# A graph network on one core: residual tiles reloaded earlier, last heads scaled one step ahead, scale weights split in another stage

## The reference, cut to what matters

```python
for i in range(4):
    y = cond_layer_norm(x, cond, s1_w[i], s1_b[i], b1_w[i], b1_b[i])      # xn * (1 + cond@sw + sb) + (cond@bw + bb)
    y = sparse_attention(y, src, dst, wq[i], bq[i], wk[i], bk[i], wv[i], bv[i], wo[i], bo[i])
    x = x + y
    y = cond_layer_norm(x, cond, s2_w[i], s2_b[i], b2_w[i], b2_b[i])
    x = x + relu(y @ m_w1[i] + m_b1[i]) @ m_w2[i] + m_b2[i]
```

## Time and profile before

| | |
|---|---|
| median of 3 runs | 1757.74 us (1755.12 to 1758.2) |
| the profiled execution: time | 1758.62 us |
| its span, first to last instruction | 1756.9 us |
| PE busy | 1718.3 us (98%) |
| DVE busy | 1210.8 us (69%) |
| ACT busy | 802.0 us (46%) |
| POOL busy | 555.4 us (32%) |
| mean granted TensorE clock | 0.995 |

### The profile page before, as it was taken

The page is one execution under the profiler, slowest core; times in us unless marked ns, Lnnn a source line. Parts: engine busy times, 40 slices in busy tenths (PEclk is TensorE's granted clock), DMA queues, the critical chain, the costliest instruction groups (busy, mean ns, idle before and its releaser), DMA issues.

```text
span 1756.9 us, 32326 instructions
## 1 busy us (share of the span) xinstructions
PE 1718.3 (98%) x11894; PEld 1516.8 (86%) x11894; DVE 1210.8 (69%) x2215; ACT 802.0 (46%) x1322; POOL 555.4 (32%) x887
## 2 busy tenths in 40 slices
PE   7999999999999999999999999999999999999998
PEld 6998788888999788889998888899988887999877
DVE  6996459457787765477777573677766836777685
ACT  4667332136666231256663412466634123666531
POOL 1002513313333722033337330233354402233473
PEclk9999999999999999999999999999999999999999
DMA  4003311311111313121113122112130312111221
GB/s 133 1 1 131 131 43 43 126 69 43 47 46 31 117 31 122 44 64 46 46 31 96 55 83 83 46 46 61 31 99 25 100 53 75 39 46 61 68 92 71
DMA packets 64714, 113.07 MB, mean 64 GB/s; under 512 B 15254, under 2 KB 25622, under 8 KB 64576
## 3 DMA queue, kind: packets, MB, share of 16 engines
q1 hardware_dynamic: 64576, 111.22, 19.3%
HBM read 89.19 MB, written 22.00 MB: 63 GB/s over the span
## 4 chain that ended last, share of the span: by engine, by line
PE 91%; DVE 4%; issue 2%; DMA 1%; POOL 1%; DVEq 1%; ACT 0%; ACTq 0%; SPq 0%; POOLq 0%
PE ps L1539 59%; PE ps L1599 15%; PE ps L1692 6%; PE ps L1489 4%; PE ps L1524 2%; PE ps L1624 2%; PE ps L1638 2%; DVE masked_s L1261 1%; DMA x<-in_x_dram 1%; DVE hot L1089 1%; DVE pT L1245 0%; DVE v_low L1229 0%; DVE x_low L1110 0%; DMA x<-x_spill 0%; PE ps L1460 0%
## 5 line engine op out<-in xcount | busy, mean ns | idle before, releaser
L1245 DVE TENSOR_TENSOR pT<-ps,pT 128x640 fp32r<-128x640 f32 (+1 forms) x320 | 243.8, 803 | 162.3 <-ACT pT L1003 162.3
L1539 PE MATMUL ps<-yT,w 128*128 128x512 f32 (+1 forms) x1728 | 330.0, 352 | 0.0
L1003 ACT CAST pT<-ps 128x640 fp32r<-128x640 f32 (+1 forms) x320 | 202.5, 685 | 259.7 <-PE ps L1692 253.8
L1539 PEld LDWEIGHTS ps<-yT,w 128*128 128x128 f32 x1728 | 280.6, 189 | 44.8
L1539 PE MATMUL ps<-kh,q_parts 128*128 128x512 f32 (+3 forms) x1440 | 312.0, 361 | 7.2 <-DVE small L1261 7.2
L1539 PEld LDWEIGHTS ps<-kh,q_parts 128*128 128x128 f32 (+1 forms) x1440 | 244.2, 186 | 53.9 <-issue 5.9
L1539 PE MATMUL ps<-w,kh 128*128 128x512 f32 (+1 forms) x960 | 237.6, 399 | 7.2 <-POOL kh L739 7.2
L1539 PEld LDWEIGHTS ps<-w,kh 128*128 128x128 f32 (+1 forms) x960 | 175.4, 187 | 47.4 <-DVE x L1363 8.0
L1599 PE MATMUL ps<-pT,v 128*128 128x256 f32 (+3 forms) x1600 | 215.6, 281 | 0.0
L940 ACT ACTIVATE s<-masked_s,small 128x1250 f32 (+1 forms) x156 | 211.3, 1354 | 0.0
L1599 PEld LDWEIGHTS ps<-pT,v 128*128 128x128 f32 (+1 forms) x1600 | 200.2, 190 | 0.0
(11 more groups left out here) (192 smaller groups left out, 2540.3 us busy)
## 6 DMA issues: line engine op xcount, KB each, us to landing
mask<-mask_dram SPq DMA_DIRECT2D x24, 640.0 KB, 5.1
x_spill<-x SPq DMA_DIRECT2D x36, 256.0 KB
x<-x_spill SPq DMA_DIRECT2D x36, 256.0 KB, 5.4
rep<-rec_dram SPq DMA_DIRECT2D x64, 128.0 KB, 3.3
w_raw<-in_L_gnn_m_w_dram SPq DMA_DIRECT2D x8, 1024.0 KB, 5.9
mask_y<-mask_dram SPq DMA_DIRECT2D x12, 640.0 KB, 5.3
mask_dram<-mask_out SPq DMA_DIRECT2D x10, 640.0 KB, 2.9
x<-in_x_dram SPq DMA_DIRECT2D x2, 2304.0 KB
```

Source lines behind the costliest of these rows:

```text
L1003: nc.scalar.copy(pT[:, 0, turned_places(gh, half), k * P:k * P + R], turn_bank(half, R)).then_inc(p_high, 1)
L1245: nc.vector.tensor_tensor(pT[:, 1, places, k * P:k * P + R], turn_bank(half, R), pT[:, 0, places, k * P:k * P + R].bitcast(F32), ALU.subtr ...
L1539: mine = mm(to, left(a), right(b), start=first and n == 0, stop=final and n == 2)
```

## The change

Four edits, none of which changes what is computed.

1. SP issues the reloads of `x` tiles 2 to 6 as soon as TensorE has read tiles 0 to 4 of V's low part for the last time, and tiles 7 to 9 after the last use of the rest (new semaphore `low_used`), instead of all eight after the last head's output was copied. The `rep` of the last head is issued between the two groups instead of ahead of them.
2. GpSimd scales the last two heads in round 2, ahead of the third root, instead of in round 3. Within a round the split of the head outputs stands first.
3. The second norm's `film` weights are loaded ahead of V's weights and split right after the first norm's last FB product, instead of at the start of attention.
4. VectorE makes the last tile of `v_low` one unit later.

```diff
@@ attention_loads @@
+                sp.wait_ge(film_ready, 2 * i + 1)
+                load_film(i, s2_w, s2_b, b2_w, b2_b)
                 sp.wait_ge(made, c.made + jl.made["Q", KD - 1, 2])
                 load_w("V", wv, i)
@@ block_loads @@
                 i = c.block
-                sp.wait_ge(film_ready, 2 * i + 1)
-                load_film(i, s2_w, s2_b, b2_w, b2_b)
                 sp.wait_ge(made, c.made)
...
                 sp.wait_ge(turned, i * U + U)
                 load_w("M1", m_w1, i)
-                spread_reciprocals(GH - 1, i)
-                sp.wait_ge(head_out, i * GH + GH)
-                for t in range(2, NT):
-                    reload_x(t)
+                for half in range(2):
+                    if half == 1:
+                        spread_reciprocals(GH - 1, i)
+                    sp.wait_ge(low_used, 2 * i + half + 1)
+                    for t in (range(2, 7), range(7, NT))[half]:
+                        reload_x(t)
@@ gpsimd, ahead of the blocks @@
             for t in range(NT):
                 add_bias(t, qkv0, zero_now, 1)
+            pool.wait_ge(made, qkv0.made["FB", NT - 1, 0])
+            split_film(1)
@@ pool_block @@
                 pool.wait_ge(made, c.made)
-                split_film(2 * i + 1)
                 pool.sem_inc(passed)
...
                 for t in range(NT + 1):
-                    if t == 3:
+                    if t + 2 < NT:
+                        split_head_outputs(t + 2, i)
+                    if t == 2:
                         scale_head_output(GH - 2, i)
                         scale_head_output(GH - 1, i)
-                    if t + 2 < NT:
-                        split_head_outputs(t + 2, i)
                     if t < NT:
                         rstd_of(t, (2 * i + 2) * NT + t)
...
+                    pool.wait_ge(made, c.made + m2_qkv.made["FB", NT - 1, 0])
+                    split_film(2 * i + 3)
                     for gh in range(2):
                         q_part(gh, i + 1)
@@ vector, attention @@
                     if u + 1 < U:
                         mask(u + 1, i)
-                    if u == 0:
+                    if u == 1:
                         v_low_part(NT - 1, i)
@@ tensor, weigh @@
+                    if gh == GH - 1 and a == 1:
+                        mine.then_inc(low_used, 1)
```

More of the change, by code:

```diff
@@ L399, in gnn_kernel @@
         x_spilled, x_back = sem("x_spilled"), [sem(f"x_back_{t}") for t in range(NT)]
+        low_used = sem("v_low_used")
         turned, p_high, p_ready, summed, head_out = sem("turned"), sem("weights_high"), sem("weights_ready"), sem("summed"), sem("head_out")
```

## The result

The changed kernel takes **1746.21 us** (median of 4 runs, 1746.05 to 1747.33) against 1757.97 us for the kernel before in the same measurement (4 runs, 1755.12 to 1759.05). The ratio is 0.9941, 95% interval 0.9929 to 0.9954: 11.8 us less, clear of noise. The forecast was 1750 us with a range of 1745.5 to 1755, so the sign was right and the time is near the low end of the range, 0.3 us under the 1746.5 us at which the prediction put it with the low clock gone in both places.

A forecast was written before the change was run, and what follows sets the result against it. PE, busy 98% of the span, bounds the kernel through its waits and low clock. From the 1757.74 us median, 6.6 us of waits (3.8 attention, 2.8 WO stage) and about 1.1 us of clock give 1750 us, range 1745.5 to 1755.

The forecast's parts named there:

- the low clock gone in both places: Range's low end, 1746.5 us: no clock drop at the start of attention or behind the WO stage's wait.
- The two terms for PE's waits: Start of attention 0.95 us a block, 3.8 us in all; WO stage before tile 5 0.7 us a block, 2.8 us.
- the term for the clock: Second block's clock drop at the start of attention avoided: 1.5 us, taken as about 1.1 us from the median.
- Rival 3: Start of attention: the wait only moves on, `v_low` slow or next mask late for `scores(4)`; 1754.3 us; 13%.
- Rival 1: WO stage: `rep` lands in time, no stall before tile 5; 1742.7 us; 8%.
- rival 2: WO stage: `rep` lands 0.7 us later than taken, the scaling eats the whole gain; 1752.4 us; 12%.
- rival 4: WO stage: last `rep` delayed past the three last tiles, longer waits and low clock; slower, 1765.8 us; 7%.
- the 0.3 us that the prediction gave the earlier reloads: WO stage: tile 2 still lands behind the M1 weights, gaining only the last `rep`'s transfer time, 0.3 us.
- The term: WO stage: PE's wait before tile 5 falls from 2.8 to 2.1 us, 0.7 us a block, 2.8 us in all.
- The 1.5 us of the second block: Start of attention: the clock drop slowing the fourth scores does not come; 1.5 us back, bounds 0 and 1.5.
- the reason given: Start of attention: two 0.7 us waits nearly 3 us apart, instead of three close together, keep the clock.
- The 2.5 us of the third block: WO stage: low clock in tile 5's product behind the 2.79 us wait; 2.5 us, in the range only.

The follow-up runs named there:

- rep_last: The changed kernel with the last head's `rep` issued behind all eight reloads of `x`: 1758.18 us, ratio 1.0009.
- wo_edits: The kernel before with only the earlier reloads and the scaling in round 2 with the split first, start of attention as before: 1751.49 us, ratio 0.9972.
- scale_late: The changed kernel with the last two heads scaled in round 3 again, ahead of the split: 1749.62 us, ratio 0.9960.
- film_only: The kernel before with only `film` loaded earlier and split in the Q products, `v_low` at its old place: 1750.74 us, ratio 0.9965.
- vlow_only: The kernel before with only the last `v_low` made one unit later, `film` still split at the start of attention: 1751.44 us, ratio 0.9968.
- attention_edits: The kernel before with both the moved `film` and the later `v_low`, WO stage as before: 1750.58 us, ratio 0.9971.

## Why the prediction was right, and where it was short

The forecast was 7.7 us of gain and 11.8 were measured. The two terms for PE's waits were right (6.6 us forecast, 6.9 measured); the term for the clock was too small (about 1.1 us in the sum, 4.2 between the two traces).

*Start of attention.* Right in mechanism and size: 0.93 us a block against 0.95. The mask is bound by `scores(2)`, the remaining wait is 0.64 us (forecast about 0.7), and `v_low` takes 0.68 us. Rival 3 did not come: the mask ahead of `scores(4)` had 0.7 us of cover, more than the 0.25 reckoned, since it followed unit 1's `pT` closer than I had it. What the prediction did not say is that the two edits there are substitutes; the runs show that either gives the whole.

*`film`.* Cost nothing, as forecast. VectorE's low part of K's weights ran its 2.28 us in the changed trace as well, since GpSimd's subtraction had ended before it began.

*Reloads and scaling.* Right in mechanism: `rep` lands right behind the fifth reload (1299.3 and 1299.7 in the third block), PE starts 4.1 us behind it, and the wait is still there in blocks 3 and 4. Rival 1 is out by the wait for `rep` in the changed trace, rival 2 by the 3.2 us gained, rival 4 needed the order of `rep_last`. The last `rep` landed 0.3 to 0.5 us behind the fifth reload in every block, so nothing overtook. In the first, second and fourth block tile 2 landed 0.6 us behind the M1 weights instead of 0.9 to 1.0, the 0.3 us that the prediction gave the earlier reloads.

The term was 2.8 us and measured 3.2, but the even 0.7 us a block is partly luck: PE's wait fell by 0.28, 1.14, 1.04 and 0.69 us. Where it fell least, the weights landed later behind their issue than before (6.9 us instead of 6.2 in the first block); where it fell most, earlier (6.2 instead of 6.5, and 6.9 instead of 8.3, in the second and third). That the weights' landing is the cause is a reading of these eight places; no run holds it fixed, and why it varies is open.

*Clock.* Here the sum was short. The 1.5 us of the second block came back as forecast. This fits the reason given: in the nine traces with two waits at the start of attention the clock fell there in none of 36 blocks, and in the two with three waits (before, `wo_edits`) in 2 of 8. The 2.5 us of the third block were left out of the sum, as open, and came back as well, 2.7 us with the small products behind. Together the clock gave 3.1 us more than the 1.1 in the sum, most of the 3.8 us between 1750 and 1746.2; the range had it.

*Low clock as a matter of length.* The prediction left open whether a wait of 2.1 us keeps the clock, and length alone does not decide it. Before tile 5's product the clock fell with waits of 1.84, 3.14 and 3.66 us (`rep_last`), 2.13 (`scale_late`), 2.73 (`film_only`), 2.79 (before) and 2.98 (`vlow_only`), and it held through waits of 2.35 (before) and 2.21 (`attention_edits`). A wait of 2.17 us lost it in `film_only` (the product took 4.58 us) and kept it in `vlow_only` (3.00 us), both in the fourth block. In the trace of `attention_edits` PE stood still for 2.76 us in the third block, and the windows of that wait and of the round behind it are at full clock:

```profile
1301.35:1304.10 2.75, 0.00 (x0) 1.00 0.01 3
1304.10:1307.80 3.70, 3.70 (x19) 1.00 0.48 140
```

So one execution of a kernel can pay and another not, and the recorded mean clock of each run shows it. The 23 runs of the kernel before that were measured beside `attention_edits` go from 1752.4 us at a clock of 0.998 to 1759.7 at 0.994. 0.4% of 1757 us is 7.0 us, the whole spread. `attention_edits` goes from 1748.1 us at 0.999 to 1755.2 at 0.995 in the same way. The changed kernel had 0.998 in all four runs. At that clock it is 5 to 7 us under the kernel before, about the 6.9 us of shorter waits; the rest of the 11.8 us is clock. What decides in a given run whether a wait loses the clock, no run here shows.

## What to carry to other kernels

When a late transfer shares a queue with a large one, issuing it earlier buys little as long as the large one stays ahead (2.6 us earlier in issue brought tile 2 about 0.3 us here); ask which byte of the queue the waiting engine needs first, and move the large transfer behind it if its reader has time. The change moved five tiles ahead of a small transfer that was needed sooner than they were, and at the same time made it needed sooner still; following that transfer from issue to landing to the product that waits found another 4 us.

Two edits aimed at the same wait should be run apart: each may already reach the next bound.

A wait of PE of two to three us cost up to twice its length here, since the clock sometimes fell with it: 2.79 us of waiting and 2.5 us of slower product in one case, 2.76 us of waiting and nothing more in another. Price it that way in the range, but not as certain. And look at the mean clock of every run before reading a difference of a few microseconds as the work of an edit.

## What was not expected of the hardware

- A VectorE subtraction with both inputs in SBUF ended 0.54 us behind the end of a GpSimd subtraction that was running when it started, with two different partners (`film`: 1.76 us in all; `q_parts`: 1.20 us), and took 0.68 us alone. The `pT` subtraction, with one input in PSUM, was not stretched beside the same `film` subtraction (1.56 us for two).
- A stand of PE of 2.76 us left the granted clock at 1.00 in one trace, and one of 1.84 us was followed by 0.50 in another; 2.17 us went both ways.
- Between blocks of one execution the M1 weights (1 MB) took 6.2 to 8.3 us from issue to landing, with the same transfers issued around them.
